# Gates made in pieces between the chunks of the first maxima pass, three more inverses made inside the attention block, and the tail's loads put in another order

## The reference

```python
mod = (silu(c) @ wmod).reshape(4, 6, 1, -1)
sa, ca, ga, sb, cb, gb = mod[:, 0..5]
ga = (2 * (ga >= 0) - 1) * maximum(abs(ga), 0.25)      # gb the same
h = layernorm(x) * (1 + ca) + sa
x = x + ga * attention(h, W_qkv, W_o)                  # causal, softmax
h = layernorm(x) * (1 + cb) + sb
x = x + gb * moe(h, router_w, w1, w2)                  # top 2 of 8 experts
```

## Time and profile before

| | us |
|---|---|
| median of 3 runs | 2805.51 |
| lowest, highest | 2802.87, 2821.97 |
| profiled execution | 2802.04 |
| span of its profile | 2800.0 |
| PE busy, share of the span | 2531.5, 90% |
| DVE busy | 2177.0, 78% |
| ACT busy | 1724.4, 62% |
| POOL busy | 692.9, 25% |

### The profile page before, as it was taken

How to read it: one execution, slowest core, us unless ns; L and a number is a source line. 1 busy time by engine, 2 the same in 40 slices (tenths; PEclk the granted TensorE clock), 3 DMA queues, 4 the chain that set the end, 5 groups by cost and what they waited for, 6 DMA issues and landing times. The chain is left out here.

```text
span 2800.0 us, 49359 instructions
## 1 busy us (share of the span) xinstructions
PE 2531.5 (90%) x16192; PEld 1296.4 (46%) x16192; DVE 2177.0 (78%) x5272; ACT 1724.4 (62%) x3477; POOL 692.9 (25%) x715
## 2 busy tenths in 40 slices
PE   6988999999999999999999999999996589999990
PEld 5871333333333333333333333333332479999990
DVE  6979888888888888888888888888822867777761
ACT  3660377777666666666666666666674257777760
POOL 2444332100010101011010110101001435556553
PEclk8995799999999999999999999999998689999995
DMA  4989778602404134040431504224013535555548
GB/s 145 317 300 276 282 279 298 192 12 71 96 28 98 49 78 119 15 114 30 95 99 31 120 28 97 62 68 105 19 49 117 186 82 91 86 92 92 90 70 253
DMA packets 217599, 331.29 MB, mean 118 GB/s; under 512 B 27024, under 2 KB 157584, under 8 KB 217360
## 3 DMA queue, kind: packets, MB, share of 16 engines
q1 hardware_dynamic: 137728, 170.68, 21.3%
q0 software_dynamic: 58512, 136.67, 19.2%
q10 hardware_dynamic: 21120, 20.97, 2.4%
HBM read 140.23 MB, written 187.20 MB: 117 GB/s over the span
## 5 line engine op out<-in xcount | busy, mean ns | idle before, releaser
L1023 ACT ACTIVATE probs<-ps 128x512 f32<-128x512 f32 (+3 forms) x2400 | 1121.2, 538 | 653.7 <-PE ps L1318 343.0
L1047 DVE TENSOR_REDUCE early<-ps 128x1 f32<-128x512 f32 x1536 | 1001.7, 684 | 108.2 <-PE ps L1235 101.7
L1235 PE MATMUL ps<-kh,qs 96*128 96x512 bf16 (+3 forms) x2560 | 890.8, 364 | 78.2 <-DVE early L1047 29.9
L1318 PE MATMUL ps<-qs,kh 99*128 99x512 bf16 (+3 forms) x2560 | 827.5, 350 | 16.5 <-ACT probs L1023 7.1
L1334 PE MATMUL ps<-probs,vs 128*32 128x512 f32 (+3 forms) x5120 | 602.3, 542 | 0.0
L1235 PEld LDWEIGHTS ps<-kh,qs 96*128 96x128 bf16 x2560 | 249.5, 99 | 698.5 <-DVE early L1047 313.4
L1043 DVE CUSTOM_DVE_ANT_0 junk<-ps,causal 128x128 bf16<-128x128 f32 (+3 forms) x1024 | 480.1, 483 | 49.0 <-PE ps L1235 44.8
L1318 PEld LDWEIGHTS ps<-qs,kh 99*128 99x128 bf16 x2560 | 245.5, 98 | 287.1 <-ACT probs L1023 135.2
L1735 POOL DMA_INDIRECT acc<-y,to x156 | 251.9, 1615 | 117.8 <-ACT y L1790 72.5
L951 POOL DMA_INDIRECT rows_out<-row,place_a x96 | 95.2, 992 | 716.2 <-DVE place_a L726 669.7
L1322 PE MATMUL ps<-ident_b,causal_b 128*128 128x128 bf16 x1024 | 213.8, 220 | 0.0
(11 more groups left out here) (230 smaller groups left out, 2997.1 us busy)
## 6 DMA issues: line engine op xcount, KB each, us to landing
rows_out<-row POOLq DMA_DIRECT2D x129, 544.0 KB, 3.6
xg<-rows_out SPq DMA_DIRECT2D x39, 544.0 KB, 3.8
v_ones<-vt SPq DMA_DIRECT2D x16, 1024.0 KB, 6.3
vs<-v_ones SPq DMA_DIRECT2D x16, 1024.0 KB, 11.5
contexts<-ctx_out SPq DMA_DIRECT2D x64, 256.0 KB
q_parts<-parts SPq DMA_DIRECT2D x32, 384.0 KB, 4.6
k_parts<-parts SPq DMA_DIRECT2D x32, 384.0 KB, 4.5
qs<-q_parts SPq DMA_DIRECT2D x64, 192.0 KB, 7.7
```

Source lines behind the costliest of these rows:

```text
L1023: nc.scalar.activation(probs[u % PB][:, h, q0:TB], bank(s % SB)[:, q0:TB], ACT.Exp, scale=SCALE).then_inc(exp_done, 1)
L1047: nc.vector.tensor_reduce(early[:, h, t, k0 // CW:k0 // CW + 1], tile, AX.X, ALU.max).then_inc(max_done, 1)
L1235: nc.tensor.matmul(tile[:, 0:w], qh[a % HR][0:STACK, t * P:(t + 1) * P], kh[a % HR][0:STACK, k0:k0 + w], start=True, stop=True).then_inc(m ...
L1318: mm = nc.tensor.matmul(tile[:, q0:TB], kh[a % HR][:, kt * P:(kt + 1) * P], qh[a % HR][:, j * TB + q0:(j + 1) * TB], start=True, stop=not ...
```

## The change

Three parts. (1) In block1 the gates are no longer made. The modulation columns alone are, behind the first transposes, and the first block's variance and normalisation come ahead of them. The gates' 16 products stand singly in pass 0 of the maxima, one in front of every eighth chunk from 14 (`GATE_ROWS`), with their half of `wmod` loaded anew by ACT; ACT copies the results, DVE applies the guard in pass 2 and takes the reciprocals in pass 3 instead of pass 1. (2) POOL and DVE also make the inverses of blocks 12, 13 and 14 in attend. (3) The tail loads `num` and `den` of block 12 first, the sums of block 15 behind them, x one block at a time, and makes `over_gate` of all four blocks at the end.

```diff
-WIDEN, MOD, GATE_INVERSE, FIRST_PLACES = 20, (30, 34, 38, 42), (60, 80, 100, 120), 140
+WIDEN, MOD, FIRST_PLACES = 20, (30, 34, 38, 42), 140
+GATE_ROWS, GATE_INVERSE = tuple(range(14, 142, 8)), (40, 70, 100, 130)
 # block1, vector
                 variance(0, 0)
-                gate_guard()
                 normalise(0, 0)
+                modulation()
                 modulate(0, 0, 0)
 # block1, tensor
+                pe.wait_ge(c_steps, 3)
+                pe.wait_ge(setup_in, 32)
...
+                pe.wait_ge(c_steps, 7)
+                pe.wait_ge(wqkv_split, 3)
 # attend, gpsimd
-                    if n + 1 < HIDDEN_BLOCKS:
-                        inverses_of(n + 1)
+                    inverses_of(n + 1)
                     name_tokens(n)
                     send(n)
                     store_over(n)
+                for n in range(HIDDEN_BLOCKS + 1, NBLK - 1):
+                    inverses_of(n)
+                pool.wait_ge(inverse_out, 16 * (NBLK - 1))
 # attend, scalar, first
+                for side, off in enumerate((2 * D, 5 * D)):
+                    act.dma_start(wmod_g[:, :, side, :], wmod[:, off:off + D].rearrange("(k p) n -> p k n", p=P)
+                                  ).then_inc(w_in, 16)
+                for b in range(B):
+                    act.wait_ge(mod_mm, b + 1)
+                    nc.scalar.activation(gates[:, b, :], bank(b), ACT.Copy).then_inc(gate_raw, 1)
 # attend, vector
+                        if g == 2 and c in GATE_INVERSE:
+                            gate_guard(GATE_INVERSE.index(c))
+                        if g == BPB - 1 and c in GATE_INVERSE:
+                            gate_inverse(GATE_INVERSE.index(c))
-                        if c == INVERT and 0 <= n + 1 < HIDDEN_BLOCKS:
+                        if c == INVERT and n + 1 >= 0:
                             invert(n + 1)
+                for n in range(HIDDEN_BLOCKS + 1, NBLK - 1):
+                    invert(n)
 # attend, tensor
+                    if g == 0 and c in GATE_ROWS:
+                        gate_rows(GATE_ROWS.index(c))
 # tail, sync
-                    if m == 0:
-                        sp.wait_ge(inverted, 1)
-                        sp.dma_start(inverses[HIDDEN_BLOCKS:NBLK].rearrange(flat, t=BPB * H * TB // P), sums[:, :]
-                                     ).then_inc(inverse_out, 16)
+                    if m == blocks[-1]:
                         sp.wait_ge(inverse_out, 16)
...
+                    if m == 0:
+                        sp.dma_start(sums[:, :], dens[NBLK - 1].rearrange(flat, t=H * TB // P)).then_inc(sums_in, 16)
+                    if m == 1:
+                        sp.wait_ge(inverted, 1)
+                        sp.dma_start(inverses[NBLK - 1].rearrange(flat, t=H * TB // P), sums[:, :]
+                                     ).then_inc(inverse_out, 16)
 # tail, scalar
+                def load_x(m):
+                    if m:
+                        act.wait_ge(ctx_in[m - 1], 32 * KK)
+                        act.wait_ge(x_in, 16 * m)
                     act.dma_start(xres[m][:, :, :], x[cols(m), :].rearrange("(t p) d -> p t d", p=P)
                                   ).then_inc(x_in, 16)
 # tail, vector
                     centre(m)
-                    if m:
-                        over_gate(m - 1)
                     modulate(m)
                     if m:
                         choose(m - 1)
                 choose(blocks[-1])
-                over_gate(blocks[-1])
+                for m in blocks:
+                    over_gate(m)
```

More of the change, by code:

```diff
@@ L245, in adaln_layer @@
         attend(nc, sb, sem, bank, x, q_parts, k_parts, v_ones, contexts, dens, inverses, rows_out, acc,
-               wo_s, rw_s, ident, mod_t, gates, w_in, keep)
+               wo_s, rw_s, ident, mod_t, gates, w_in, keep, silu, wmod)
         w1_raw = sb("w1_raw", [P, KK, E, W])
@@ L427, in _ @@
                 root(0, 0)
+                act.wait_ge(setup_in, 32)
+                nc.scalar.activation(wqkv_hi[:, :, :], wqkv_s[:, :, :], ACT.Copy).then_inc(wqkv_split, 1)
                 load(0, 1)
@@ L620, in _ @@
                 transposes(0, 0)
+                pe.wait_ge(c_steps, 3)
+                pe.wait_ge(setup_in, 32)
+                for w, which in enumerate((0, 1, 3, 4)):
+                    for half in range(KK):
+                        for k in range(KK):
+                            c0 = which * D + half * P
+                            n0 = (w * KK + half) * B
+                            mm = nc.tensor.matmul(bank(4)[:, n0:n0 + B], wmod_s[:, k, c0:c0 + P],
+                                                  silu[:, k, :], start=(k == 0), stop=(k == KK - 1))
+                mm.then_inc(mod_mm, 1)
+                pe.wait_ge(c_steps, 7)
+                pe.wait_ge(wqkv_split, 3)
                 last = NBLK // 2 - 1
@@ L730, in attend @@
 def attend(nc, sb_, sem, bank, x, q_parts, k_parts, v_ones, contexts, dens, inverses, rows_out, acc,
-           wo_s, rw_s, ident, mod_t, gates, w_in, keep):
+           wo_s, rw_s, ident, mod_t, gates, w_in, keep, silu, wmod):
     with ExitStack() as own:
@@ L753, in attend @@
         work = [sb(f"work{k}", [P, KK * TB]) for k in range(4)]
+        wmod_g = work[2][:, :].rearrange("p (k g d) -> p k g d", k=KK, g=2)
+        silu_all = work[3][:, :].rearrange("p (k b q) -> p k b q", k=KK, b=B)
+        sign, size = (work[2][:, n * 2 * D:(n + 1) * 2 * D] for n in range(2))
         sums = sb("sums", [P, H * TB // P])
@@ L1500, in _ @@
             def _(dve):
-                dve.wait_ge(sums_in, 16)
-                nc.vector.reciprocal(sums[:, :], sums[:, :]).then_inc(inverted, 1)
                 def normalise_contexts(m):
@@ L1519, in residual @@
                 def residual(m):
[L1520 removed]
+                    dve.wait_ge(x_in, 16 * (m + 1))
                     for half in range(2):
@@ L1573, in _ @@
                 normalise_contexts(0)
+                dve.wait_ge(sums_in, 16)
+                nc.vector.reciprocal(sums[:, :], sums[:, :]).then_inc(inverted, 1)
                 for m in blocks:
```

114 lines of the change are left out of this document (48 added, 66 removed).

## The result

The changed kernel takes 2791.9 us (median of 5, 2788.6 to 2797.8) where the kernel before took 2805.7 beside it: ratio 0.9945, 95% interval 0.9919 to 0.9970. A second measurement on another chip gave 0.9949 (0.9932 to 0.9967). It is faster by 14 us, half of what was forecast, and 2 us above the range.

A forecast was written before the change was run, and what follows sets the result against it. It took DVE to bound pass 0, PE the steps, and waiting chains the start and tail. -16.1 + 0.3 + 0.5 + 2.0 + 0.6 - 8.5 + 0.5 - 3.0 = -23.7 from 2802.0 gave 2778 us, range 2769 to 2790.

The forecast's parts named there:

- the tail keeps its wait: Rival, chance 0.14: the tail's 8-engine transfers crowd each other and attend ends 4 us later; -12.8 in all, 2789 us.
- Start of block1: Block1's start: without the gates in the chain, first query product at 23.9 instead of 39.98; -16.1 us (-14.3 to -18.0).
- 5.5, since the transposes have just run: Block1's start: the 32 modulation instructions cost 3.63 to 7.3 us depending on PE's speed; 5.5 taken.
- First head: Start of attend: ACT's two `wmod` loads, 0.5 MB, issued ahead of SP's heads, cost +0.3 us (0 to 1.5).
- Gate products: Pass 0 of the maxima: the 16 products, 12.8 us of PE, stay hidden under DVE; +0.5 us (0 to 12.8).
- The rival with step 0 starting at full speed: Second way within a rival of chance 0.20: gate products release PE's clock in pass 0, some 4 us won; -27.7, 2774 us.
- Guard: Step 1 of attend: DVE's guard in four bursts of about 2.0 us costs +2.0 us (0 to 8.1).
- Reciprocals: Attend: four reciprocals of 1.74 us move from step 0 (-1.7 us) to step 2 (+1.7 us).
- End of attend: End of attend: POOL, with inverses of blocks 13 and 14 behind the last scatter, ends about as late; +0.6 us (0 to +4).
- Tail: Tail: earlier `num` and `den` loads -8.5 us (-4 to -12), one late pair +0.5, middle and end -3.0.
- The second pair 6 us later: Tail: the second block's `num` and `den`, 1.05 MB, come 6 us after the first, at 2156.5 instead of 2164.98.
- 0.20 and two fifths of 0.55: Chance of over 1% faster, given as 0.41: rival of more gain (2773 or 2774 us) 0.20, forecast's own range (2773 to 2784) 0.55.

The follow-up runs named there:

- the run with the end only: The kernel before with only the changed kernel's rounds of inverses and tail; start, gates, guard and reciprocals as before: ratio 0.9966 to the kernel before.
- the run with `wmod` behind it: The changed kernel with ACT's two `wmod` loads issued only after attend's first head landed, gate products 16 chunks later: ratio 0.9929 to the kernel before.

## Why the prediction was wrong, step by step

**What failed** are terms of the sum, nearly all in the same direction: the guard's bursts (+3.1 over the forecast), the tail's second pair (+2.9), the first head (+2.6), the rounds at the end of attend (+2.4) and the modulation instructions at the start (+1.7). The path is the forecast's in every stretch, but the reasons for four of these sizes were wrong: how far PE's lead covers DVE, what a transfer on another queue costs (twice), and what eight transposes do to PE's clock. No rival came about as a whole; of "the tail keeps its wait" one half did, attend ending 3.0 later for its 4, and not the other, a tail shorter by only 4. 10.4 us lie between the sums of the table, and 3.5 more between the profiled execution that the sum was made against and the median of before. The likeliest number was given on the base of the one profile, though its distance to the median was known; the clock losses now show what such a distance can be made of: on record the kernel before takes 2797 to 2802 us at its highest mean granted clock, 0.948, and 2828 at its lowest, 0.937.

- **Start of block1, -16.1:** the order was right, 13.4 for the forecast's 13.2. "5.5, since the transposes have just run" failed: eight transposes behind an idle PE don't raise the clock. They ran at half speed themselves (1.94 us, for 1.06 at full), and the 32 products behind them near the upper bound of 7.3, at 6.96. Against the start in the run with the end only the saving would be 16.1, the forecast's, so the total is no surer than the 1.65 us between the two starts of before; the 6.96 is sure. My reading of the earlier trace rows was right that the clock column shows 1.00 where PE runs at half speed; it does so in the changed kernel's profile too, beside the 6.96.
- **First head, +0.3:** measured 2.9, outside its bounds of 0 to 1.5. "SP's own order of issue sets when the first head lands" failed; the run with `wmod` behind it gives 2.65 back. Half a megabyte is 2 us at the 252 GB/s of that stretch before (198 to 214 us), and 1.8 at the 285 GB/s of the earlier trace rows: even by that row the upper bound of 1.5 was too low.
- **Gate products, +0.5:** right, 0.4, but in part by luck. The sum put 58.0 us of columns against DVE's 84.0, where the earlier trace rows has PE busy for 77.2; with the 12.8 of the products that would be 90.0. In the changed kernel PE was busy 73.4 with the products in it, at a higher clock. What they cost at 0.50 throughout is not shown. The clock rose in parts of pass 0, to a mean of 0.66 for 0.50 in the earlier trace rows; step 0 still took 109.9, 0.8 less than the forecast. The rival with step 0 starting at full speed and 4 us won didn't come. Of the rule in the Trainium skill (TensorE: Matmul & The Clock Gate, Part 1) that activity releases the throttle the trace shows this much and no gain in time, since DVE sets the pass.
- **Guard, +2.0:** measured 5.1, the largest miss, though inside its bounds. Two steps failed: a burst is 2.28 us, not 2.03, and of it PE's lead covers 1.0, not the 1.3 that follow from the reciprocals of the earlier trace rows. Even by those the sum would have been 4 x (2.03 - 1.3) = 2.9: the 2.0 was a guess below its own rows. That the same 1.3 did hold for the reciprocals in step 2 says that a lead read from one kind of burst, at one place, doesn't carry over to another.
- **Reciprocals, -1.7 and +1.7:** -2.5 (with the rise of the clock in it) and +1.9.
- **End of attend, +0.6:** measured 3.0. That POOL would end near SP was right; I had it level, and it was 3 behind. The forecast's own times give 9.8 us from the issue of the store to `acc` to the landing of the last store of inverses; it took 12.2, the store issued until 2142.7 landing 1.7 later. Left out were the 0.54 us in which POOL issues each store and the 0.3 from each reciprocal to it, and a load took 1.95 for 1.7; the first round, beside the 0.5 MB store to `acc`, took 3.2 us from the load at 2133.03 to the reciprocal. The +0.6 had no row behind it at all.
- **Tail, -8.5 + 0.5 - 3.0:** measured -8.3. The first pair came at 11.2, near the forecast's 10.6. "The second pair 6 us later" failed: 8.2, for x moves beside it. It would have been 5.2 without x. The middle and the end gave -2.7 for -2.5, right: `place` of m = 2 came 3.7 earlier behind the second normalise, the last scatter 1.0 later behind `place`.
- **Range:** 2790 lies 12 us above the sum. The bad ends of start, first head, guard, end of attend and tail lie 17 above it (1.8 + 1.2 + 6.1 + 3.4 + 4.5), and the base added 3.5. Terms that were all taken nearer their good end don't cancel. (Of the chances, 0.20 and two fifths of 0.55 make 0.42, not 0.41.)

## What to carry to other kernels

Work that is moved under cover of another engine should be cut to the length of that engine's lead: 9 us cost 1.2 in 16 pieces and 5.1 in 4. A transfer beside the one that everything waits for cost its bytes here, though issued on another queue (0.5 MB: 2.6 us once, 3 the other time); and an engine that issues loads under waits must have nothing behind them that is needed soon. When a sum is made from one profile, first measure steps that should be alike: what they differ by is the clock's, and it can be as large as the change. And take a second profile of the same kernel before a difference of 2 or 3 us in a stretch is read as an effect.

## What the runs showed of the hardware

- Granted clock of one core alone: 11 like steps took 119.3 to 119.7 us without a dip and up to 122.0 or 123.9 with, in all 1.6 to 28.7 us of a profiled execution, which can be more than the change is worth. The changed kernel took 2785.4 to 2792.0 us at a mean clock of 0.955 to 0.957 and 2791.8 to 2800.2 at 0.951 to 0.954.
- The clock column is no evidence at the start of a profile: 1.00 beside 217 ns for an instruction, 0.50 beside the same 217 ns in another kernel's profile. The duration of a known instruction tells (113 ns at full speed). The Trainium skill (TensorE: Matmul & The Clock Gate, Part 1) warns that such clock events can be unreliable; this trace agrees in so far as 1.00 stands where PE ran at half speed.
- PE can do eight transposes at full speed (1.06 us) after 3.1 us of idling and be at half speed directly behind them (32 products in 6.96 us).
